# A decoder layer's tail as its own program: tiles pipelined, sums on TensorE

## What is computed

```python
x = x + attn(layernorm(x), Wq, Wk, Wv, Wo)      # 16 heads of 32, causal over 512 tokens
x = x + xattn(layernorm(x), ctx, ctx)
x = x + ffn(layernorm(x), kernel, bias, a, b)   # x @ quantised(kernel) + bias + (x @ a) @ b

def xattn(q, k, v):                             # per token: 16 heads attend to 16 heads
    scores = einsum('bsqd,bskd->bsqk', q, k) / 4        # q, k of 16 heads x 16
    scores = where(tril(ones(16, 16)), scores, -1e18)
    return einsum('bsqk,bskd->bsqd', softmax(scores), v)
```

## Time and profile before

| | us |
|---|---|
| median of 3 runs | 851.5 (850.72 to 851.78) |
| profiled execution, its own time | 852.45 |
| its span, first to last instruction | 850.6 |
| PE busy | 692.9 (81%) |
| DVE busy | 662.9 (78%) |
| POOL busy | 522.9 (61%) |
| ACT busy | 399.7 (47%) |
| mean granted TensorE clock | 0.923 |

### The profile page before, as it was taken

One profiled execution on the slowest core, in us unless ns is written; L12 is line 12 of the kernel. 1 busy time (PEld: TensorE's weight loads), 2 busy tenths in 40 slices (PEclk: granted clock), 3 DMA queues, 4 the chain that ended last, 5 costly groups with the idle time before them and its releaser, 6 DMA issues.

```text
span 850.6 us, 14919 instructions
## 1 busy us (share of the span) xinstructions
PE 692.9 (81%) x5099; PEld 461.3 (54%) x5099; DVE 662.9 (78%) x1204; ACT 399.7 (47%) x754; POOL 522.9 (61%) x434
## 2 busy tenths in 40 slices
PE   3688999999999999999999999999999978330023
PEld 2465655755575566665656576657665644320023
DVE  3544455467878987999799879987888799899973
ACT  5123555365636573647364646464645465210201
POOL 5000000034848896878687877788778878867961
PEclk9779999999999999999999999999999999675555
DMA  6876566677757775767566766675667601100000
GB/s 184 111 90 101 79 93 86 106 95 94 96 101 95 92 95 103 92 106 92 90 97 104 94 102 90 102 98 83 81 111 99 86 8 32 38 6 31 0 25 25
DMA packets 47927, 70.46 MB, mean 83 GB/s; under 512 B 4849, under 2 KB 22530, under 8 KB 47874
## 3 DMA queue, kind: packets, MB, share of 16 engines
q1 hardware_dynamic: 46850, 69.52, 54.7%
q10 hardware_dynamic: 1024, 0.26, 0.1%
HBM read 14.98 MB, written 4.19 MB: 23 GB/s over the span
## 4 chain that ended last, share of the span: by engine, by line
PE 53%; DVE 21%; DMA 14%; issue 6%; ACT 3%; POOL 1%; SPq 1%; ACTq 0%; DVEq 0%; POOLq 0%
PE misc L438 23%; DMA stack_k<-k_lo 14%; PE acc_bank L438 9%; PE max_bank L438 9%; PE exp_bank L438 8%; DVE head_out L930 4%; DVE head_scores L930 3%; DVE neg_max L918 2%; DVE x L1030 2%; PE sum_bank L438 2%; DVE prod L313 2%; DVE seg_max L918 1%; DVE ln_raw L896 1%; DVE x2t_lo L1050 1%; SPq L385 1%
## 5 line engine op out<-in xcount | busy, mean ns | idle before, releaser
L733 ACT ACTIVATE probs<-exp_bank 128x512 f32<-128x512 f32 x320 | 188.4, 592 | 202.0 <-PE exp_bank L438 199.3
L1192 POOL TENSOR_TENSOR prod<-head_probs,ctx_sb 128x256 f32<-128x256 f32 (+3 forms) x128 | 236.7, 1883 | 21.3 <-DVE head_out L930 19.3
L918 DVE TENSOR_REDUCE neg_max<-max_bank 128x1 f32<-128x512 f32 (+1 forms) x192 | 130.6, 683 | 91.6 <-PE max_bank L438 91.0
L313 POOL TENSOR_TENSOR prod<-x1n,ctx_sb 128x256 f32<-128x256 f32 (+2 forms) x112 | 175.3, 1595 | 4.3 <-ACT x1n L693 4.3
L438 PE MATMUL max_bank<-stack_k,stack_q 96*128 96x384 f32 (+3 forms) x512 | 156.7, 369 | 18.9 <-DMA stack_k<-k_lo 9.8
L438 PE MATMUL acc_bank<-probs,values 128*32 128x512 f32 (+3 forms) x1024 | 157.4, 445 | 4.1 <-ACT log_sum L748 2.1
L438 PE MATMUL sum_bank<-probs,ones 128*32 128x512 f32 (+3 forms) x1024 | 156.8, 442 | 0.0
L438 PE MATMUL exp_bank<-stack_q,stack_k 97*128 97x384 f32 (+3 forms) x512 | 150.0, 355 | 2.5 <-DVE wf_lo L888 1.3
L1125 POOL TENSOR_TENSOR ln_var<-ln_mv,eps 128x4 f32<-128x4 f32 x24 | 5.3, 219 | 209.9 <-DVE ln_mv L904 209.9
L438 PEld LDWEIGHTS exp_bank<-stack_q,stack_k 97*128 97x128 f32 x512 | 84.2, 194 | 56.6 <-issue 27.5
L918 DVE TENSOR_REDUCE seg_max<-max_bank 128x4 f32<-128x512 f32 x128 | 86.8, 682 | 28.2 <-PE max_bank L438 26.7
(11 more groups left out here) (116 smaller groups left out, 1222.8 us busy)
## 6 DMA issues: line engine op xcount, KB each, us to landing
stack_q<-q_hi SPq DMA_DIRECT2D x64, 256.0 KB, 5.6
stack_k<-k_hi SPq DMA_DIRECT2D x64, 256.0 KB, 9.5
stack_q<-q_lo SPq DMA_DIRECT2D x32, 256.0 KB, 7.0
stack_k<-k_lo SPq DMA_DIRECT2D x32, 256.0 KB, 10.7
x_in<-in_x SPq DMA_DIRECT2D x8, 512.0 KB, 5.2
ctx_sb<-in_ctx SPq DMA_DIRECT2D x32, 128.0 KB, 3.3
x<-in_x SPq DMA_DIRECT2D x8, 512.0 KB, 10.1
out<-y_sb SPq DMA_DIRECT2D x8, 512.0 KB, 3.2
```

The costliest lines, as they stand in the source:

```text
L313: last = engine.tensor_tensor(qk_prod[:, COFF[j]:COFF[j + 1]].rearrange("p (q k d) -> p q k d", q=4, d=HD), x1n[:, t, 4 * j * HD:4 * (j + ...
L733: nc.scalar.activation(probs[:, (UNITS * g + n) % PTR, :], exp_bank[n % 2][:, :], ACT.Exp, scale=SCALE).then_inc(exp_done, 1)
L918: vec.tensor_reduce(o, v, axis=AX_X, op=ALU.max, negate=True).then_inc(max_taken, 1)
L1192: last = gp.tensor_tensor(pv_prod[:, COFF[j]:COFF[j + 1]].rearrange("p (q d k) -> p q d k", q=4, k=keys), head_probs[:, 4 * j:4 * j + 4, N ...
```

## The change

The bodies end with iteration 7, and each engine then runs a program of its own for what is left: token tiles 1 to 3 of batch 6 (called 1 to 3) and the four of batch 7 (4 to 7), with tile 0 of batch 6 finished first. The rules for late tiles are gone, so in groups 2 and 3 of iteration 7 POOL again makes all products.

In the end program ScalarE writes context and normalised x of a tile with the dimension outermost (`turn_context`, `last_layernorm1`). VectorE multiplies dimensions 0 to 11, POOL 12 to 15. TensorE adds the 16 products of each pair by matmuls with the identity into a PSUM bank that begins with the mask. VectorE takes maxima and subtracts from PSUM. Value products are laid out by key; VectorE makes those of keys 0 to 7, POOL those of 8 to 15, and TensorE adds over the keys, again with the identity. The score sums of tile u + 1 stand ahead of the value sums of tile u in TensorE's program. The second normalisation and feed-forward of the last three batches run on halves of two tiles, with the bias added by a matmul on TensorE, and six stores of half a batch. The x of the last batch is kept in `x_in`, not `x1`.

```diff
-        for i in range(after, n_batch + 3):
+        for i in range(after, n_batch):
...
-        LATE_VECTOR, LATE_POOL = (3, 0), (1, 2)
-        FIRST_LATE = NG * N_BATCH - 2
...
+        POOL_DIMS, VECTOR_DIMS = (12, HD), ((0, 6), (6, 12))
+        POOL_KEYS, VECTOR_KEYS = (2, 3), (0, 1)
...
+        score_sum_bank, value_sum_bank = exp_bank
+        last_wo_bank, end_y_bank = max_bank, (acc_bank, sum_bank)
...
+        def end_score_products(engine, u, dims):
+            d0, d1 = dims
+            for j in range(CHUNKS):
+                keys = 4 * (j + 1)
+                last = engine.tensor_tensor(
+                    end_prod_qk[:, d0:d1, COFF[j] // HD:COFF[j + 1] // HD].rearrange("p d (q k) -> p d q k", q=4),
+                    end_x1n_turned(u)[:, d0:d1, 4 * j:4 * j + 4, None].to_broadcast([P, d1 - d0, 4, keys]),
+                    end_ctx_turned(u)[:, d0:d1, None, 0:keys].to_broadcast([P, d1 - d0, 4, keys]), ALU.mult)
+            return last
+        def end_value_products(engine, u, j):
+            queries = NH - 4 * j
+            return engine.tensor_tensor(
+                end_prod_pv[:, KOFF[j]:KOFF[j + 1]].rearrange("p (k q d) -> p k q d", k=4, d=HD),
+                end_probs[u % 2][:, 4 * j:NH, 4 * j:4 * j + 4].rearrange("p q k -> p k q")[:, :, :, None]
+                .to_broadcast([P, 4, queries, HD]),
+                end_ctx(u)[:, 4 * j * HD:4 * (j + 1) * HD].rearrange("p (k o d) -> p k o d", o=1, d=HD)
+                .to_broadcast([P, 4, queries, HD]), ALU.mult)
...
+            for t in range(NT):
+                if t == 0:
+                    sp.wait_ge(hpv_prod, n_pv.now() + 1 - NT)
+                else:
+                    sp.wait_ge(end_pv_vector, 2 * t)
+                    sp.wait_ge(end_pv_pool, t)
+                sp.dma_start(ctx_sb[:, t, :], ctx_t[LAST, :, t, :]).then_inc(ctx_loaded[t], 16)
...
+            def end_score_sums(u):
+                wait(pe, end_shifted, u - 2)
+                for j in range(CHUNKS):
+                    mm(score_sum_bank[:, COFF[j] // HD:COFF[j + 1] // HD], ident_b[:, :],
+                       head_mask[:, 4 * j:4 * j + 4, 0:4 * (j + 1)], start=(j == 0), stop=False, skip_group_check=True)
+                pe.wait_ge(end_qk_pool, u - 1)
+                dims = list(range(*POOL_DIMS))
+                for n, part in enumerate(VECTOR_DIMS):
+                    for d in dims:
+                        mm(score_sum_bank[:, 0:PAIRS], ident[:, :], end_prod_qk[:, d, :], start=False, stop=False,
+                           skip_group_check=True)
+                    pe.wait_ge(end_qk_vector, 2 * (u - 2) + n + 1)
+                    dims = list(range(*part))
+                for d in dims:
+                    last = mm(score_sum_bank[:, 0:PAIRS], ident[:, :], end_prod_qk[:, d, :], start=False,
+                              stop=(d == dims[-1]), skip_group_check=True)
+                last.then_inc(end_qk_sum, 1)
+            def end_value_sums(u):
+                wait(pe, end_added, u - 1)
+                for j in VECTOR_KEYS + POOL_KEYS:
+                    if j in VECTOR_KEYS:
+                        pe.wait_ge(end_pv_vector, 2 * (u - 1) + j + 1)
+                    if j == POOL_KEYS[0]:
+                        pe.wait_ge(end_pv_pool, u)
+                    width = (NH - 4 * j) * HD
+                    for k in range(4):
+                        last = mm(value_sum_bank[:, C - width:C], ident[:, :],
+                                  end_prod_pv[:, KOFF[j] + k * width:KOFF[j] + (k + 1) * width],
+                                  start=(j == 0 and k == 0), stop=(j == CHUNKS - 1 and k == 3), skip_group_check=True)
+                last.then_inc(end_pv_sum, 1)
...
+            end_score_sums(2)
+            end_value_sums(1)
+            end_transpose(0)
+            end_transpose(1)
+            for u in range(2, 2 * NT):
+                if u + 1 in END_TILES:
+                    end_score_sums(u + 1)
+                if u == 7:
+                    end_transpose(4)
+                end_value_sums(u)
+                if u == 2:
+                    end_ffn(0)
+                    end_ffn(1)
...
+            def end_maxima(u):
+                dve.wait_ge(end_qk_sum, u - 1)
+                for j in range(CHUNKS):
+                    last = vec.tensor_reduce(head_max[:, 4 * j:4 * j + 4], ragged(j), axis=AX_X, op=ALU.max)
+                own(last)
+                if u == 2:
+                    dve.wait_ge(end_preset, 1)
+                else:
+                    dve.wait_ge(end_exp, u - 1)
+                for j in range(CHUNKS):
+                    last = vec.tensor_tensor(
+                        end_shift[:, 4 * j:4 * j + 4, 0:4 * (j + 1)], ragged(j),
+                        head_max[:, 4 * j:4 * j + 4, None].to_broadcast([P, 4, 4 * (j + 1)]), ALU.subtract)
+                last.then_inc(end_shifted, 1)
+            def end_normalise(u):
+                probs_u = end_probs[u % 2]
+                dve.wait_ge(end_exp, u)
+                own(vec.tensor_reduce(head_sum[:, :], probs_u, axis=AX_X, op=ALU.add))
+                own(vec.reciprocal(head_inv[:, :], head_sum[:, :]))
+                vec.tensor_tensor(probs_u, probs_u, head_inv[:, :, None].to_broadcast([P, NH, NH]),
+                                  ALU.mult).then_inc(end_normal, 1)
+                dve.wait_ge(end_normal, u)
+                wait(dve, end_pv_sum, u - 1)
+                for j in VECTOR_KEYS:
+                    end_value_products(vec, u, j).then_inc(end_pv_vector, 1)
...
+            end_vector_scores(2)
+            last_normalise()
+            end_first_tile()
+            end_normalise(1)
+            last_add_to_x1(0)
+            last_add_to_x1(1)
+            for u in range(2, 2 * NT):
+                end_maxima(u)
+                if u + 1 in END_TILES:
+                    end_vector_scores(u + 1)
+                end_add(u - 1)
+                end_normalise(u)
+                if u == 2:
+                    end_low_part(0)
+                    end_low_part(1)
+                    end_statistics(2)
...
+            def end_pool_values(u):
+                pool.wait_ge(end_normal, u)
+                if u == 1:
+                    pool.wait_ge(hpv_sum, n_pv.now())
+                wait(pool, end_pv_sum, u - 1)
+                for j in POOL_KEYS:
+                    last = end_value_products(gp, u, j)
+                last.then_inc(end_pv_pool, 1)
...
```

More of the change, by code:

```diff
@@ L667, in body, with last_projection_most @@
                             ffn(n - 7)
+            def last_projection_most():
+                pe.wait_ge(attn_ready, NG * N_BATCH - 1)
+                pe.wait_ge(max_taken, n_max_bank.now())
+                for half in (0, 1):
+                    for t in (0, 1):
+                        tok = (2 * half + t) * P
+                        for k in range(NG - 1):
+                            mm(last_wo_bank[half][:, t * C:(t + 1) * C], attn_t[:, k, tok:tok + P], wo_sb[:, k, :],
+                               start=(t == 0 and k == 0), stop=False, skip_group_check=True)
@@ new lines, in end_transpose @@
+            def end_transpose(v):
+                half = v % 2
+                pe.wait_ge(end_x2n, v + 1)
+                if v == 0:
+                    pe.wait_ge(y_ready, CC * (N_BATCH - 3))
+                wait(pe, end_x2t_lo, v - 1)
+                for c in range(CC):
+                    for t in (0, 1):
+                        last = nc.tensor.transpose(misc[half][:, (2 * c + t) * P:(2 * c + t + 1) * P],
+                                                   x2n[:, 2 * half + t, c * P:(c + 1) * P], ident[:, :])
+                last.then_inc(end_x2t_psum, 1)
@@ L1086, in body, with half_statistics @@
                         other_weights()
+            def half_statistics(which, src, half, done):
+                for n in (0, 1):
+                    last = vec.bn_stats(ln_raw[:, which, 2 * half + n, :], src[:, n, :])
+                own(last)
+                vec.tensor_copy(touched[:, which, :], ln_raw[:, which, 2 * half, 0:1])
+                for n in (0, 1):
+                    last = vec.bn_aggr(ln_mv[:, which, 2 * half + n, :], ln_raw[:, which, 2 * half + n, :])
+                last.then_inc(done, 1)
@@ L1197, in body @@
                         last.then_inc(hpv_prod, 1)
-                    if scored and not late(i, g):
+                    if scored:
                         pool.wait_ge(hqk_sum, n_sum.up())
```

355 lines of the change are left out of this document (296 added, 59 removed).

## The result

The changed kernel takes **828.35 us** (median of 4 runs, 827.4 to 829.5) beside 851.64 for the kernel before in the same runs (ratio 0.9717, 95% interval 0.9698 to 0.9735): 23.3 us less, where 26 were forecast. 828.35 lies 2.85 above the prediction. The profiled execution took 829.26 us for a span of 827.4.

What follows compares the result with a forecast made beforehand. VectorE was taken to bound the last 128 us; entry to 740.0, six tiles 68.4, end 9.65, store 3.4 and clock 3 gave 824.4 against 850.6. Taking 26 from the 851.5 median gave 825.5 us, range 818 to 841.

Steps and rivals of the forecast that it cites:

- What lies ahead stays alone: Before the tail: the change leaves this part nearly alone, with the last attention matmuls ending at 722.6 us as before.
- the rival of the held attention: Attention's end: POOL reaches its products later and ScalarE's exponentials queue, up to 6 us, giving 831.5; chance 0.08.
- POOL's two groups: Groups 2 and 3 of the last batch: POOL makes all products, 15.6 us each, last old-style shift done by 725.3.
- VectorE's entry: Start of the end program: VectorE works 13.4 us from 725.0 plus 1.6 of waits; first new maxima at 740.0.
- TensorE sets the pace: Six tiles: TensorE, at 11.0 us per tile, is the bound; with 0.4 for two long periods, 68.4 us to 808.4.
- the allowance of 0.8: TensorE's cost per tile: 0.8 us added for pipe drains at handovers and 64-column matmuls held by their loads.
- VectorE 8.5 us per tile: End program: VectorE's remaining work per tile, 7.3 us plus 1.2 of half work, is 8.5 us.
- Series of VectorE and POOL: Six tiles: if nothing of POOL's reading overlaps VectorE, a tile costs 13.4 us, giving 837.5; chance 0.20.
- Weight loads in series: TensorE's sums: no weight load hides, adding 12.5 us per tile at 0.195 each, giving 900; chance 0.02.
- Clock, 3 us for two falls: Holes of the entry, waiting for products of tiles 1 and 3: two clock falls cost 3 us, bounds 0 and 6.
- The end: After the six tiles: last addition, statistics, transposes, feed-forward half and result take 9.65 us, from 808.4 to 818.0.
- The store: Last store, now half the size: kept at 3.4 us, to 821.4; earlier stores are hidden.

Runs made afterwards that it cites:

- e11: Changed kernel with POOL's end-program products replaced by one-column memsets, so sums take old data; VectorE's instructions unchanged: 825.44 us.
- e6: On top of e1_pool_free, feed-forward bias of each half made two float32r matmuls, placed ahead of the wait for the low part: 820.76 us.
- e2: Changed kernel with half of the end program's identity matmuls left out, all products still made: 816.83 us.
- e4_filler: Changed kernel with twenty useless matmuls on TensorE before the last transposes and twenty before the last feed-forward half: 824.49 us.
- e5_control: The changed kernel run again without any change: 826.83 us.
- e8_f32r: End program's products rounded to float32r in the attention's stacks, identity sums as single float32r matmuls, against the changed kernel: 825.84 us.
- e1_pool_free: Changed kernel with VectorE making all products of the end program and POOL only the coefficients: 825.60 us.
- e10_all: e6 plus useless matmuls where TensorE waits at entry and end, tile 2's score products and the logarithms' factors moved earlier: 818.94 us.

## Why the prediction was right, step by step, and where not

- **What lies ahead stays alone**: this step failed in the profiled execution, where the mark comes 3.41 us later. The attention's last matmul ended at 725.6 instead of 722.6, but 28.7 us behind the mark where it was 29.2: the rival of the held attention is out, and 2.2 of the 3.4 us are there by the first exponentials (58.38 for 56.14). The account closes: 25.8 us from the mark, plus 0.8 of the store, less 3.4, is 23.2, the difference of the two profiled executions (852.45 - 829.26). On the mean of all traces the mark is 2.2 us late, which would be most of the 2.85 that the median lies above the forecast; whether those 2.2 belong to the change stays open, as said under the kernel before.
- **POOL's two groups**: forecast 31.2 us to the end of the last shift, measured 729.87 - 697.51 = 32.4.
- **VectorE's entry**: 15.0 us forecast, 14.5 measured (728.87 to 743.35). The terms were off and cancelled: value products 3.00 for 2.1 and score products 3.05 for 2.6, and waits near 0 for the 1.6 charged. What POOL costs VectorE in value products shows as longer instructions, not as waits.
- **TensorE sets the pace**: right from the second period on, by e11, e6 and the 20.00 of 20 us busy; the first is VectorE's, by e2. Sums 9.3 us with the mask matmuls and without the drain for 8.8, half work 1.7 for 1.4 (a bias matmul of one row and 256 columns takes 0.62 us with its gap, not 0.43); the allowance of 0.8, made for drains and loads, took both in, and that is luck.
- **VectorE 8.5 us per tile**: too low. It was 9.7 (period of 11.29 less 1.60 idle) to 10.2 (10.81 less 0.57), and 11.2 in the first period. The products alone were right to 0.05 us; the stretch beside POOL was left out of the sum. TensorE's 11 us hid it.
- **Series of VectorE and POOL (0.20)**: its premise is true and its price wrong. The value products do follow one another, but little else does; coefficients ran under other work, and 10.2 us of VectorE still fit under TensorE's 11.
- **Weight loads in series**: out, at 9.35 us for 64 records, where loads in a row at 0.195 us would add 12.5. By the rule of the Trainium skill, "TensorE: Matmul & The Clock Gate", section on packing small matmuls, it would be an estimate of 6.8 more; the trace does not agree. A floor per record does show, below.
- **Clock, 3 us for two falls**: the sum was near, by luck, since the places were not those named. The entry had none in the profiled run (1.6 us in e4_filler's trace); the end had one, 2.6 us, in a half that the prediction had priced at full clock. **The end** was 12.6 us for 9.65 mostly because of it. **The store** took 827.4 - 824.81 = 2.6 us for 3.4.

## What to carry to other kernels

Before work is shared between VectorE and GpSimd, look whether both read two SBUF inputs: here the share was no relief (3.00 us for 1792 elements beside POOL, 3.03 for all 2560 alone), and the cheaper engine could have all of it. When TensorE takes over sums, the order in its one queue can be worth more than the whole change (34.6 us against 25.8 here); put what frees the other engine first. Compare two kernels from a mark that both pass, or a shift at the start is booked on the change, and take both traces from one chip.

## What the runs showed of the hardware that was not expected

- The granted clock fell from 1.00 to 0.50 with TensorE busy without a gap, inside a feed-forward half with its one-row bias matmuls, at 783 us in e5_control and at 804 in e11_alone. In e8_f32r it stayed at 0.50 through two such halves in a row, but also from 780 to 800, where some 15 of 20 us are float32r sums. In e6_bias, whose bias matmuls are shorter, it stayed 1.00 from 740 to 800. That the bias is the cause wasn't shown.
- Behind a wait of 2.78 us the eight records of the projection took 3.49 us (e1_pool_free), behind one of 1.60 us 1.99 (changed kernel). The length of the wait does not decide it alone: behind waits of 2.43 us for POOL's products of tile 3, 64 records took 9.37 us in the changed kernel and 11.05 in e4_filler. So the same wait costs clock in one execution and not in another.
- Sixteen float32r identity matmuls of 256, 192, 128 and 64 columns start (1.93 - 0.16) / 16 = 0.111 us apart on the mean at full clock (e8_f32r), hardly closer than feed-forward's of 256, 0.119; fewer columns helped little. bf16 matmuls of 128 columns start 2.40 / 40 = 0.06 apart (e10_all).
